# Keys and first centring by token in 64x64 quarters of the array, in two rounds with the banks exchanged between them

## The chip, the core and the metric

The kernel runs on one core of one Trainium2 chip. The metric is the device time of one execution, in microseconds (us). Before the change three executions took 1174.82, 1178.27 and 1172.48 us, so the median is 1174.82 us. Lower is better.

## What is computed

The reference takes 32 images of 64 channels and 32 x 32 pixels, and applies three blocks one after the other. The parts that matter here are the layer norm that stands ahead of attention, and the keys:

```
x = x + conv_block(group_norm(x))            # gated 1x1 convolutions
t = tokens(x)                                # 1024 tokens of 64 features per image
u = (t - mean(t)) / sqrt(var(t) + 1e-5)      # per token, over its 64 features
q, k, v = u @ Wq, u @ Wk, u @ Wv             # 64 x 64 weights
Q, K = elu(q) + 1, elu(k) + 1
KV = sum over tokens of K (x) v, per head    # linear attention, 8 heads
t = t + (u + layernorm(relu([u, msg] @ W1) @ W2))       # msg = layernorm(attended @ Wm)
t = t + mixture_of_8_experts(layernorm(t))   # top 2 of 8, each 64 -> 128 -> 64, GELU
```

All of it is in 32-bit floats but for a few constants.

## The kernel before, in words

Two images lie on the 128 partitions together: image 0 of a pair on partitions 0 to 63, image 1 on 64 to 127, a feature per partition and 1024 tokens in the free dimension. Such a pair is a slot, two slots make a group, and there are 8 groups. A slot's matrix results go to one tensor R0 or R1, two PSUM banks of 512 columns each; the experts use two tensors of their own, HP0 and HP1.

The work is software-pipelined over groups. The steady list SCHEDULE names the dense stages of group a (convolution, attention, hidden layers, router), and between them it sets units of the experts of group a-1. For each unit TensorE runs a first layer (L847), ScalarE the GELU (L992), TensorE a second layer (L861), VectorE the weighting (L1355) and GpSimd the addition to the sum (L1044). Each engine walks the same list in order, so the list fixes the order on every engine, and semaphores fix the times. Group 0 and the convolution of group 1 (called EARLY in the code) have another list, OPENING, in which no expert unit stands. Groups 2 to 7 go through the steady list from their convolution on, groups 1 to 7 from the keys on.

Two stages make a result that is laid out by token, with 128 tokens on the partitions and 2 x 64 features in the columns. They do so by holding 128 x 128 of the data as weights and moving a 128 x 128 matrix past it, which has the 64 x 64 weights of both images on its diagonal and zeros elsewhere:

- `centre_1` (L699 by the helper `by_token`) subtracts each token's mean. It waits for VectorE's sum x1 (L1163), half a slot at a time. ScalarE squares the result (L945), VectorE adds the squares up (L1184), takes the reciprocal root in some ten short steps (L1190 on), and scales (L1210). The result is turned back to features by TensorE (L641).
- `key` makes the keys. It first fills half a slot with ones (L681, from bf16 constants, so that the result is k + 1), then adds the keys (L708), and waits half by half for VectorE's finished queries (L1243), because both lie in R. ScalarE takes the exponential (L958), VectorE the minimum and maximum (again L1243), and `key_value` (L717) starts when both halves of the slot's keys are done.

A 32-bit matmul of the program is two pairs of a weight load and a matmul record in the trace, each pair for half of its passes. Where a matmul uses 64 rows or 64 columns of the array, others can run in the rest of it. The query stage (L692) does this already with four quarters.

Of the kernel before, what the change touches and what calls it, by code (L numbers as in the profile page):

```python
# [10 lines left out]
BF16 = mybir.dt.bfloat16  # L11
ALU = mybir.AluOpType
ACT = mybir.ActivationFunctionType
AX_X = mybir.AxisListType.X

P = 128
C = 64
# [5 lines left out]
CH = 512  # L23
NCH = T // CH
# [32 lines left out]
NQ = CH // P  # L57
# [73 lines left out]
def build(nc, x, wpack, w1e, reps, out):  # L131
    xd = x.rearrange("(n two) c t -> n (two c) t", two=2)
    od = out.rearrange("(n two) c t -> n (two c) t", two=2)
    with ExitStack() as ctx:
        def sb(name, shape, dt=F32):
            return ctx.enter_context(nc.sbuf_tensor(name, shape, dt))
# [4 lines left out]
        def sems(name):  # L141
            return [sem(f"{name}{g}") for g in range(G)]
# [5 lines left out]
        XN = sb("XN", [P, G, T])  # L148
# [22 lines left out]
        SPAN = sb("SPAN", [P, NQ, P])  # L171
        BH = sb("BH", [P, 1])
        BT = sb("BT", [P, 1])
        ONE = sb("ONE", [P, 2], BF16)
        MINUS = sb("MINUS", [P, 1])
        BI = sb("BI", [P, 2, 2])
        W1E = sb("W1E", [P, E, HID])
# [7 lines left out]
        R = [psum(f"R{s}", T) for s in range(G)]  # L185
# [5 lines left out]
        def w(name, rows=slice(0, P)):  # L191
            a, n = COLS[name]
            return W[rows, a:a + n]
# [10 lines left out]
        def half(c):  # L204
            return slice(c * CH, (c + 1) * CH)
# [16 lines left out]
        def img(k):  # L222
            return slice(k * C, (k + 1) * C)
# [42 lines left out]
        x1_done = sems("x1_done")  # L266
        ln_ps = sems("ln_ps")
# [4 lines left out]
        xn_back = sems("xn_back")  # L272
        xs_done = sems("xs_done")
        msg_norm = sems("msg_norm")
        qk_ps = sems("qk_ps")
        qk_exp = sems("qk_exp")
        one_set = sem("one_set")
        qk_done = sems("qk_done")
# [28 lines left out]
        xf_done = sems("xf_done")  # L307
# [25 lines left out]
        def pieces(slots):  # L333
            return [(s, c) for s in slots for c in range(NCH)]
# [11 lines left out]
        def at(n, c):  # L346

            return (n - 1) * NCH + c + 1

        LAST = NCH - 1  # L350
# [209 lines left out]
        def _(pe):  # L560
            mm = nc.tensor.matmul
# [10 lines left out]
            def parts(a, b, par):  # L572
# [52 lines left out]
                def blocks(c):  # L625

                    return range(c * TB // NCH, (c + 1) * TB // NCH)

                def centre_1(slots):
                    for s, c in pieces(slots):  # L630
                        pe.wait_ge(x1_done[s], at(a + 1, c))
                        if a == EARLY:
                            pe.wait_ge(xf_done[s], at(a, c))
                        by_token(s, c, Xa, w("center")).then_inc(ln_ps[s], 1)

                def features_1(slots):

# [41 lines left out]
                def one_everywhere(s, c):  # L679

                    mm(R[s][:, half(c)], ONE[:, 1:2].broadcast_to([P, P]), ONE[:, 0:1].broadcast_to([P, CH]), start=True, stop=False)  # L681

# [10 lines left out]
                                          start=False, stop=True)  # L693
                            last.then_inc(qk_ps[s], 1)

                def by_token(s, c, src, weights):

                    for j in blocks(c):
                        last = mm(R[s][:, P * j:P * j + P], src[:, s, P * j:P * j + P], weights,  # L699
                                  start=True, stop=True)  # L700
                    return last

                def key(slots):
                    for s, c in pieces(slots):
                        pe.wait_ge(qk_done[s], at(a * 2 + 1, c))
                        one_everywhere(s, c)
                        for j in blocks(c):
                            last = mm(R[s][:, P * j:P * j + P], XN[:, s, P * j:P * j + P], w("wk"),  # L708
                                      start=False, stop=(j == blocks(c)[-1]))
                        last.then_inc(qk_ps[s], 1)  # L710

                def key_value(slots):
                    for s in slots:
# [180 lines left out]
        def _(act):  # L894
# [5 lines left out]
            f(BT[:, :], BI[:, 1, 0:1], ACT.Copy, scale=0.5).then_inc(act_prep, 1)  # L900
            act.wait_ge(act_prep, 2)
            f(ONE[:, 0:1], BI[:, 0, 0:1], ACT.Copy, bias=1.0, scale=0.0)
            f(ONE[:, 1:2], BI[:, 0, 0:1], ACT.Copy, bias=1.0 / P, scale=0.0).then_inc(one_set, 1)

            def parts(a, b, par):
# [558 lines left out]
```

## Time and profile before

| | |
|---|---|
| median of the runs, us | 1174.82 |
| span of the profiled execution, us | 1171.7 |
| TensorE busy | 1058.5 us, 90% |
| VectorE, ScalarE, GpSimd busy | 63%, 55%, 31% |
| mean granted TensorE clock | 0.985 |
| centring records L699 | 256, in 8 stretches |
| key records L708, fill records L681 (queries' fill too) | 256, 64 |

Of the profiled execution the trace gives the span, from the first instruction to the last; the runs' times are taken around the whole execution, and their median is 3.1 us longer. The span, and each stage in it, is what the rows speak of. The stages of groups 2 to 7 repeat every 138.2 us to within 0.02 us, so one group stands for six.

### The profile page before, as it was taken

What the parts mean: (1) busy time and instruction counts of PE and PEld (TensorE: products, weight loads), DVE (VectorE), ACT (ScalarE), POOL (GpSimd) and SP (SyncE); (2) the same over time, 40 slices, a digit from 0 to 9 for tenths busy, and PEclk for the clock granted to TensorE, in tenths of its full rate; (3) what the DMA queues carried; (4) which work ended last, traced back from release to release, by engine and by line L of the source; (5) the groups of instructions that cost most, each with busy time, mean ns of one, the idle gap of its engine ahead of it and who ended that gap; (6) DMA issues with size and microseconds to landing.
All of it is one profiled execution on the core that took longest, in us unless ns stands there. A gap on an engine that the chain in (4) does not pass through costs nothing.

```text
span 1171.7 us, 16823 instructions
## 1 busy us (share of the span) xinstructions
PE 1058.5 (90%) x6646; PEld 442.3 (38%) x6646; DVE 740.2 (63%) x1529; ACT 641.8 (55%) x866; POOL 361.7 (31%) x280
## 2 busy tenths in 40 slices
PE   4798589979999899988999899998999989998898
PEld 1453244323533245332453235432453324532232
DVE  5744745686647875587664966468764886556344
ACT  3345355654566556664556546556556555665454
POOL 0000031333323333333232333133332342324465
PEclk9989889999999999999999999999999999999999
DMA  5000086007700284005810068000850039200760
GB/s 157 6 1 1 1 179 149 3 22 173 169 1 19 54 189 104 1 19 112 185 50 1 19 149 198 1 19 19 194 134 1 18 69 201 42 1 19 179 145 23
DMA packets 15597, 88.62 MB, mean 76 GB/s; under 512 B 3488, under 2 KB 6816, under 8 KB 11424
## 3 DMA queue, kind: packets, MB, share of 16 engines
q1 hardware_dynamic: 15520, 87.57, 32.3%
q8 instruction: 52, 0.85, 0.3%
q14 instruction: 25, 0.20, 0.1%
HBM read 78.12 MB, written 9.44 MB: 75 GB/s over the span
## 4 chain that ended last, share of the span: by engine, by line
PE 74%; DVE 12%; ACT 9%; issue 3%; DMA 1%; DVEq 0%; POOL 0%; POOLq 0%; SPq 0%
PE HP L847 15%; PE HP L861 14%; ACT H L992 5%; PE R L646 5%; PE R L621 4%; PE R L610 4%; PE R L699 3%; PE R L717 2%; PE R L708 2%; PE R L786 2%; PE R L795 2%; PE R L788 2%; PE R L861 2%; PE R L675 2%; DVE TM L1355 2%
## 5 line engine op out<-in xcount | busy, mean ns | idle before, releaser
L1044 POOL TENSOR_TENSOR XB<-TM,XB 128x512 f32<-128x512 f32 x254 | 323.0, 1286 | 658.5 <-DVE TM L1355 658.5
L992 ACT ACTIVATE H<-HP,W 128x1024 f32<-128x1024 f32 x224 | 243.0, 1116 | 205.7 <-PE HP L847 205.1
L1355 DVE SCALAR_TENSOR_TENSOR TM<-HP,B2S,CWB 128x512 f32<-128x512 f32 x224 | 163.2, 742 | 207.1 <-PE HP L861 196.3
L847 PE MATMUL HP<-XF,W1E 64*128 64x512 f32 x1024 | 269.9, 630 | 19.3 <-DVE TM L1355 18.5
L861 PE MATMUL HP<-H,W 128*64 128x512 f32 x896 | 233.1, 616 | 18.0 <-ACT H L992 18.0
L847 PEld LDWEIGHTS HP<-XF,W1E 64*128 64x128 f32 x1024 | 84.1, 187 | 143.9 <-DVE TM L1355 71.0
L861 PEld LDWEIGHTS HP<-H,W 128*64 128x64 f32 x896 | 48.5, 135 | 171.2 <-ACT H L992 116.3
L1156 DVE SCALAR_TENSOR_TENSOR BIG<-R,T 128x512 f32<-128x512 f32 x112 | 69.5, 681 | 20.9 <-PE R L610 20.8
L930 ACT ACTIVATE T<-R 128x512 f32<-128x512 f32 x96 | 57.4, 598 | 39.8 <-PE R L646 31.4
L958 ACT ACTIVATE T<-R,MINUS 128x512 f32<-128x512 f32 x64 | 41.4, 688 | 27.3 <-PE R L708 24.4
L1243 DVE SCALAR_TENSOR_TENSOR BIG<-T,R 128x512 f32<-128x512 f32 x64 | 41.8, 684 | 21.6 <-ACT T L958 21.6
L610 PE MATMUL R<-IM,REP 32*128 32x512 f32 x336 | 50.2, 482 | 5.1 <-ACT T L918 2.3
L621 PE MATMUL R<-BIG,W 128*64 128x512 f32 x224 | 53.0, 617 | 1.9 <-DVE BIG L1156 1.9
L975 ACT ACTIVATE BIG<-R,BH 128x512 f32<-128x512 f32 x64 | 40.5, 683 | 21.7 <-PE R L788 21.7
L1035 POOL TENSOR_TENSOR XB<-XN,X 128x1024 f32<-128x1024 f32 x14 | 33.2, 2396 | 54.9 <-ACT XN L953 54.9
L992 ACT ACTIVATE BIG<-HP,W 128x1024 f32<-128x1024 f32 x32 | 33.9, 1110 | 26.0 <-PE HP L847 26.0
L1355 DVE SCALAR_TENSOR_TENSOR TM<-R,B2S,CWB 128x512 f32<-128x512 f32 x32 | 24.0, 751 | 37.8 <-PE R L861 35.1
L924 ACT ACTIVATE T<-R,W 128x512 f32<-128x512 f32 x28 | 19.2, 687 | 45.5 <-PE R L621 45.5
L1163 DVE TENSOR_TENSOR X<-X,T 128x512 f32<-128x512 f32 x28 | 21.6, 773 | 32.4 <-ACT T L924 32.4
L1218 DVE SCALAR_TENSOR_TENSOR T<-R,T 128x512 f32<-128x512 f32 x64 | 40.4, 682 | 1.9 <-PE R L675 1.7
L918 ACT ACTIVATE T<-R 128x512 f32<-128x512 f32 x56 | 29.1, 602 | 21.4 <-PE R L610 21.3
L610 PEld LDWEIGHTS R<-IM,REP 32*128 32x128 f32 x336 | 21.7, 202 | 48.1 <-issue 19.6
(179 smaller groups left out, 1411.3 us busy)
## 6 DMA issues: line engine op xcount, KB each, us to landing
CWB<-gates_hbm SPq DMA_DIRECT2D x32, 1536.0 KB, 20.4
CWB<-gates_hbm SPq DMA_DIRECT2D x32, 512.0 KB, 6.6
out<-XB SPq DMA_DIRECT2D x15, 512.0 KB, 3.0
X<-x SPq DMA_DIRECT2D x14, 512.0 KB, 3.8
XF<-x SPq DMA_DIRECT2D x2, 512.0 KB, 6.1
gates_hbm<-RT SPq DMA_DIRECT2D x16, 64.0 KB, 1.6
W<-wpack SPq DMA_DIRECT2D x1, 968.0 KB, 4.9
W1E<-w1e SPq DMA_DIRECT2D x1, 512.0 KB, 7.4
```

The costliest lines, as they stand in the source:

```text
L610: last = mm(Ra[s][:, half(c)], REP[rows, n, :], IM[rows, s, part, :], start=(part == 0), stop=(part == 1))
L621: last = mm(Ra[s][img(k), half(c)], w("ow")[:, C * h:C * h + C], BIGa[:, s, 2 * k + h, half(c)], start=(h == 0), stop=(h == 1))
L646: return mm(R[s][:, half(c)], weights, src[:, s, half(c)], start=True, stop=True)
L847: last = mm(HP[u % BATCH][:, half(k)], W1E[img(k), e, :], XF[img(k), 1 - par, s, half(c)], start=True, stop=True)
L861: last = mm(sums_of(b, u)[img(k), :], w("w2e")[:, C * e:C * e + C], activated(b, u)[:, k, :], start=True, stop=True)
L930: f(T2[:, s, half(c)], R[s][:, half(c)], ACT.Square).then_inc(ln_sq[s], 1)
L958: f(T1[:, s, half(c)], R[s][:, half(c)], ACT.Exp, bias=MINUS[:, :]).then_inc(qk_exp[s], 1)
L992: f(activated(b, u).rearrange("p k t -> p (k t)"), HP[u % BATCH][:, :], ACT.Gelu, bias=col(B1E + e))\
L1044: nc.gpsimd.tensor_tensor(acc, TM[:, u % BATCH, :], acc, ALU.add).then_inc(acc_done, 1)
L1156: v.scalar_tensor_tensor(out=BIGa[:, s, 2 * k + h, half(c)], in0=Ra[s][:, half(c)], scalar=1.0, in1=T2a[:, s, half(c)], op0=ALU.add, op1=A ...
L1243: v.scalar_tensor_tensor(out=dst[s][:, half(c)], in0=T1[:, s, half(c)], scalar=1.0, in1=R[s][:, half(c)], op0=ALU.min, op1=ALU.max).then_i ...
L1355: v.scalar_tensor_tensor(out=TM[:, u % BATCH, :], in0=sums_of(b, u), scalar=B2S[:, e % 2, e // 2:e // 2 + 1], in1=CWB[:, s, e, half(c)], o ...
```

## The change

`by_token` now works on a whole slot, in quarters of the array. A matmul holds 64 tokens of one image (64 x 64) and moves that image's own 64 x 64 weights. Eight blocks of 128 tokens, two images and two halves of a block make 32 matmuls per slot instead of 8 of 128 x 128. In the first of two rounds image 0 (array rows 0 to 63) writes the first bank of R and image 1 (rows 64 to 127) the second; in the second round the banks are exchanged. Between the rounds TensorE waits for its own last matmul of the first round, by a new semaphore. Both callers now wait for both halves of a slot before they begin, and both halves of the result are announced together at the end. The fill of the keys is done in quarters as well, with a new constant 1/64.

```
                 def centre_1(slots):
-                    for s, c in pieces(slots):
-                        pe.wait_ge(x1_done[s], at(a + 1, c))
+                    for s in slots:
+                        pe.wait_ge(x1_done[s], at(a + 1, LAST))
                         if a == EARLY:
-                            pe.wait_ge(xf_done[s], at(a, c))
-                        by_token(s, c, Xa, w("center")).then_inc(ln_ps[s], 1)
+                            pe.wait_ge(xf_done[s], at(a, LAST))
+                        by_token(s, Xa, w("center"), c1_first[s], True).then_inc(ln_ps[s], NCH)
...
-                def by_token(s, c, src, weights):
-                    for j in blocks(c):
-                        last = mm(R[s][:, P * j:P * j + P], src[:, s, P * j:P * j + P], weights,
-                                  start=True, stop=True)
+                def by_token(s, src, weights, first_round, alone):
+                    for turned in range(2):
+                        if turned:
+                            pe.wait_ge(first_round, a + 1)
+                        for q in range(NQ):
+                            for k in range(2):
+                                at_block = P * (NQ * (k ^ turned) + q)
+                                for n in range(2):
+                                    last = mm(R[s][img(n), at_block + C * k:at_block + C * k + C],
+                                              src[img(k), s, at_block + C * n:at_block + C * n + C], weights[img(k), img(k)],
+                                              start=alone, stop=alone or (turned == 1 and q == NQ - 1))
+                        if not turned:
+                            last.then_inc(first_round, 1)
                     return last
                 def key(slots):
-                    for s, c in pieces(slots):
-                        pe.wait_ge(qk_done[s], at(a * 2 + 1, c))
-                        one_everywhere(s, c)
-                        for j in blocks(c):
-                            last = mm(R[s][:, P * j:P * j + P], XN[:, s, P * j:P * j + P], w("wk"),
-                                      start=False, stop=(j == blocks(c)[-1]))
-                        last.then_inc(qk_ps[s], 1)
+                    for s in slots:
+                        pe.wait_ge(qk_done[s], at(a * 2 + 1, LAST))
+                        for c in range(NCH):
+                            for n in range(2):
+                                mm(R[s][img(n), half(c)], ONE[img(c), 2:3].broadcast_to([C, C]), ONE[img(c), 0:1].broadcast_to([C, CH]),
+                                   start=True, stop=False)
+                        by_token(s, XN, w("wk"), key_first[s], False).then_inc(qk_ps[s], NCH)
...
+            f(ONE[:, 2:3], BI[:, 0, 0:1], ACT.Copy, bias=1.0 / C, scale=0.0)
```

On TensorE, in the steady list, the keys stood like this before, from the first wait for the queries of slot 1 to the sum of keys times values (L681 fill, L708 keys, L717 keys times values; a semaphore's name ends in its slot):

```order
L681 MATMUL R<-ONE 128x512 [waits qk_done1]
L708 MATMUL R<-W,XN 128x128 x4
L681 MATMUL R<-ONE 128x512 [waits qk_done1]
L708 MATMUL R<-W,XN 128x128 x4
L681 MATMUL R<-ONE 128x512 [waits qk_done0]
L708 MATMUL R<-W,XN 128x128 x4
L681 MATMUL R<-ONE 128x512 [waits qk_done0]
L708 MATMUL R<-W,XN 128x128 x4
L717 MATMUL R<-BIG 128x130 [waits ones_set1,qk_done1]
```

The same place on TensorE in the changed kernel (L720 fill, L708 again the keys, L729 keys times values):

```order
L720 MATMUL R<-ONE 64x512 [waits qk_done1]
L720 MATMUL R<-ONE 64x512 x3
L708 MATMUL R<-W,XN 64x64 x16
L708 MATMUL R<-W,XN 64x64 [waits key_first1]
L708 MATMUL R<-W,XN 64x64 x15
L720 MATMUL R<-ONE 64x512 [waits qk_done0]
L720 MATMUL R<-ONE 64x512 x3
L708 MATMUL R<-W,XN 64x64 x16
L708 MATMUL R<-W,XN 64x64 [waits key_first0]
L708 MATMUL R<-W,XN 64x64 x15
L729 MATMUL R<-BIG 128x130 [waits ones_set1,qk_done1]
```

Per slot there are 32 small matmuls for 8, 4 fills for 2, one wait for the queries for two, and a wait on the engine itself in the middle. The first centring in the steady list, on TensorE, before (L699 the centring, L847 the next expert layer):

```order
L699 MATMUL R<-W,X 128x128 [waits x1_done1]
L699 MATMUL R<-W,X 128x128 x3
L699 MATMUL R<-W,X 128x128 [waits x1_done1]
L699 MATMUL R<-W,X 128x128 x3
L699 MATMUL R<-W,X 128x128 [waits x1_done0]
L699 MATMUL R<-W,X 128x128 x3
L699 MATMUL R<-W,X 128x128 [waits x1_done0]
```

And after, up to the expert layer that follows (L859):

```order
L708 MATMUL R<-W,X 64x64 [waits x1_done1]
L708 MATMUL R<-W,X 64x64 x15
L708 MATMUL R<-W,X 64x64 [waits c1_first1]
L708 MATMUL R<-W,X 64x64 x15
L708 MATMUL R<-W,X 64x64 [waits x1_done0]
L708 MATMUL R<-W,X 64x64 x15
L708 MATMUL R<-W,X 64x64 [waits c1_first0]
L708 MATMUL R<-W,X 64x64 x15
L859 MATMUL HP<-XF,W1E 128x512 [waits comb_done,xf_done0]
```

No stage changes its place among the others, on any engine. ScalarE has one more instruction, for the constant, at the start.

## Rows read from the trace of the kernel before

**Rows 1.** The page: span, busy time, and the chain that ended last.

```profile
span 1171.7 us, 16823 instructions
...
PE 1058.5 (90%) x6646; PEld 442.3 (38%) x6646; DVE 740.2 (63%) x1529; ACT 641.8 (55%) x866; POOL 361.7 (31%) x280
...
PE 74%; DVE 12%; ACT 9%; issue 3%; DMA 1%; DVEq 0%; POOL 0%; POOLq 0%; SPq 0%
```

**Rows 2.** Timeline, TensorE, first centring: start us, length us, instruction, count, idle before.

```profile
289.95 3.84 PE L699 MATMUL R<-W,X 128*128 128x128 f32 x32
293.72 1.99 PE L847 MATMUL HP<-XF,W1E 64*128 64x512 f32 x8
296.06 2.08 PE L861 MATMUL HP<-H,W 128*64 128x512 f32 x8 [0.36 <-ACT H L992]
298.14 1.25 PE L641 MATMUL R<-W,BIG 128*128 128x128 f32 x8
```

**Rows 3.** The same stretch on VectorE and ScalarE.

```profile
290.79 0.69 DVE L1163 TENSOR_TENSOR X<-X,T 128x512 f32<-128x512 f32 x1 [0.65 <-ACT T L924]
...
293.83 0.60 ACT L945 ACTIVATE T<-R 128x512 f32<-128x512 f32 x1 [0.30 <-PE R L699]
...
294.46 0.69 DVE L1184 TENSOR_REDUCE SM<-T 128x8 f32<-128x512 f32 x1 [0.21 <-ACT T L945]
...
297.39 1.29 DVE L1210 TENSOR_TENSOR BIG<-R,SM 128x512 f32<-128x512 f32 x2
```

**Rows 4.** Timeline, TensorE, from the keys to the keys times values.

```profile
308.72 0.39 PE L681 MATMUL R<-ONE 128*128 128x512 bf16 x1
308.94 1.05 PE L708 MATMUL R<-W,XN 128*128 128x128 f32 x8
...
313.15 3.75 PE L717 MATMUL R<-BIG 128*128 128x130 f32 x32
```

**Rows 5.** The same stretch on ScalarE and VectorE, queries first.

```profile
305.55 2.42 ACT L958 ACTIVATE T<-R,MINUS 128x512 f32<-128x512 f32 x4
...
310.04 0.69 ACT L958 ACTIVATE T<-R,MINUS 128x512 f32<-128x512 f32 x1 [2.06 <-PE R L708]
...
307.52 2.47 DVE L1243 SCALAR_TENSOR_TENSOR BIG<-T,R 128x512 f32<-128x512 f32 x4
310.76 0.69 DVE L1243 SCALAR_TENSOR_TENSOR BIG<-T,R 128x512 f32<-128x512 f32 x1 [0.77 <-ACT T L958]
...
314.08 0.69 DVE L1243 SCALAR_TENSOR_TENSOR BIG<-T,R 128x512 f32<-128x512 f32 x1 [0.42 <-ACT T L958]
```

**Rows 6.** One line each: durations in ns (min/median/max), first and last start.

```profile
L708 PE MATMUL R<-W,XN x256: 272/275/275, 63.3 to 1004.1; 128*128 128x128 f32 x128
...
L675 PE MATMUL R<-BIG,SPAN x32: 270/270/372, 336.0 to 336.9; 32*128 32x128 f32 x32
...
L728 PE MATMUL R<-T,W x4: 169/210/250, 317.1 to 318.5; 128*128 128x1 f32 x4
...
L692 PEld LDWEIGHTS R<-XN,W x16: 129/131/133, 303.1 to 304.7; 64*64 64x64 f32 x16
L692 PE MATMUL R<-XN,W x16: 589/614/641, 303.1 to 305.1; 64*64 64x512 f32 x16
```

**Rows 7.** Timeline, TensorE, cut off at 336.05 us: L675's records begun by then.

```profile
336.03 0.39 PE L675 MATMUL R<-BIG,SPAN 32*128 32x128 f32 x4 [0.15 <-DVE BIG L1206]
```

**Rows 8.** Timeline of the queries on TensorE, in quarters.

```profile
303.08 1.09 PE L692 MATMUL R<-XN,W 64*64 64x512 f32 x8
304.10 0.61 PE L681 MATMUL R<-ONE 128*128 128x512 bf16 x2
```

**Rows 9.** Timeline of group 0, centring: TensorE, VectorE's x1, and its last sum.

```profile
45.10 3.84 PE L699 MATMUL R<-W,X 128*128 128x128 f32 x32
...
45.82 1.29 DVE L1163 TENSOR_TENSOR X<-X,T 128x512 f32<-128x512 f32 x2
...
49.61 0.69 DVE L1184 TENSOR_REDUCE SM<-T 128x8 f32<-128x512 f32 x1 [0.21 <-ACT T L945]
```

**Rows 10.** Timeline of group 0, keys times values, on TensorE.

```profile
68.31 3.75 PE L717 MATMUL R<-BIG 128*128 128x130 f32 x32
```

More of the change, by code:

```diff
@@ L173, in build @@
         BT = sb("BT", [P, 1])
-        ONE = sb("ONE", [P, 2], BF16)
+        ONE = sb("ONE", [P, 3], BF16)
         MINUS = sb("MINUS", [P, 1])
@@ L274, in build @@
         msg_norm = sems("msg_norm")
+        c1_first = sems("c1_first")
+        key_first = sems("key_first")
         qk_ps = sems("qk_ps")
```

## The prediction, made before the changed kernel ran

> **What bounds the kernel now.** I read the page's busy shares and chain first, then the timeline of the two stages on three engines, then single lines for what a small matmul costs. TensorE is busy 1058.5 of 1171.7 us, and the chain that ended last is 74% TensorE, 12% VectorE and 9% ScalarE [rows 1]. So most of what TensorE saves should count, but not all: near both changed stages the chain leaves TensorE. The first centring of a steady group runs 32 records in a row, from 289.95 until L847 follows at 293.72 [rows 2]. Behind it VectorE works without a pause from the last sum of squares (294.46) through the root steps to L1210 at 297.39, whose first half releases L641 at 298.14 [rows 2, 3]. TensorE has then just ended L861, so at L641 the two paths are about even. The keys take TensorE from 308.72 to 313.15, again without a gap [rows 4]; exponential and minimum/maximum follow each half, and the last half's VectorE step starts at 314.08 [rows 5], hidden today behind L717 of the other slot.
>
> **TensorE's own time.** In today's keys a half slot is 1.11 us (308.72 to 313.15 is four of them): a fill of 0.22 (308.72 to 308.94) and 8 records in 0.89, so 111 ns per record of 128 moved columns [rows 4]; centring is 32 such records, 3.57 us and the change to the next tiling. After the change a slot has 64 records of 64 columns, four at a time. If the quarters really run together, four records take what one record of 64 columns takes, half of 111: 56 ns. That they can is seen in the queries: 8 records of 512 columns in four quarters need 1.02 us (303.08 to 304.10), where one after the other each would be 4 x 111 ns, 3.6 us in all [rows 4, 8]. A weight load of 64 x 64 lasts 131 ns as a record [rows 6], but overlaps in the same way. What no row shows is the rate at which the sequencer delivers: 56 ns for four pairs is 14 ns per pair. Bounds: four neighbours in different row strips start within 23 ns of each other (336.03, with the cut at 336.05), at most 8 ns apiece [rows 7], and over 32 records L675 ran at 28 ns each (0.9 us from first to last start) [rows 6]. In the latter the array itself was the limit (111 ns for four), so 28 is a bound from above, no measured limit of delivery. I take 14, since neighbours at 8 ns show that pairs can come faster, and keep 28 for the range.
>
> The Trainium skill speaks against this value. Its page "TensorE: Matmul & The Clock Gate", section "Wait — 56ns, not 53.3ns?", says that starts never come closer than about 25 ns however small the matmul, and that with hardware decode off about 62 ns go to each. The trace has four starts within 23 ns, so as a distance between neighbours the 25 does not hold here; as a mean rate over many records no row refutes it. By 62, L675 could hardly have kept 28. By 25 the round would take 0.80 us instead of 0.45; what that does to the time is the second rival.
>
> The wait between the rounds: the last record of round 1 must finish. A record of 128 columns lasts 275 ns and one of a single column 169, so one of 64 some 222 [rows 6]. Release takes 0.03 to 0.04 us (ScalarE ends at 310.73, VectorE starts at 310.76 [rows 5]). Then the first load isn't hidden: L692's first records are 52 ns longer than its others (641 to 589) [rows 6]. From the last start of round 1 to the first of round 2: 0.31 us. Nothing else is in flight; L847 and all stages behind it wait with it. Below, the cost can hardly be under 0.22 (the record itself); above I allow 0.6. A round is 7 x 56 + 20 = 0.41 us from first to last start, so from a slot's first record to its last 1.13, its result is there at 1.35, and the next slot can start at 1.18. Fill for a slot: four bf16 matmuls in four quarters, 0.22 for 0.44. Per group TensorE then needs 2.36 for 3.57 (centring) and 2.80 for 4.43 (keys), 2.8 us less, 23 us over 8 groups. That is not what arrives.
>
> **Keys, steady group.** The queries' four VectorE steps start at 307.52 and are 0.60 apart, so slot 1's second half ends at 308.80 [rows 5]. Today TensorE starts at 308.72 on the first half; now at 308.84. Fill to 309.06, last record starts at 310.20, result at 310.42. ScalarE 310.46, its second half 0.58 later (four in 2.42 [rows 5]); VectorE 311.18 and 311.78, end 312.47. L717 is released at 312.51 with an unhidden load of 0.10 (first L675 records 372 for 270 ns [rows 6]), so effectively 312.61. TensorE has the second slot's keys done by about 311.65 (its queries ended at 309.99, in time) and waits 0.8 us: the wait that replaces the work. Today L717 is at 313.15, so **0.54 us earlier**, not 1.6. Slot 0's keys end on VectorE at 313.9, before L717 of slot 1 ends at 314.4. The change of tiling ahead of L717 falls into that wait. Everything behind L717 follows in order, so I let the 0.54 pass on. Seven groups: 3.8 us.
>
> **First centring, steady group.** Slot 1 starts as today at 289.95, since both its halves were ready, and ends at 291.13. Slot 0 now waits for its second half: VectorE ends at 291.48 [rows 3], a new idle 0.4 us. First record effectively at 291.57, result at 292.92. ScalarE's second half then starts near 293.47 (0.51 behind the first, an estimate from 0.60 each with overlap), VectorE's second sum at 294.20 (two, 0.60 apart, from 293.59), against 294.46 [rows 3]: **0.26 us earlier**. TensorE's own L847 starts 0.9 us sooner but meets the GELU behind ScalarE's squares, and L641 needs L1210. Six groups: 1.5 us.
>
> **Opening.** Group 0's centring: slot 1's x1 is done at 45.82 + 1.29 = 47.11 [rows 9]; start 47.2, result 48.57, last sum from 49.84 instead of 49.61 [rows 9]: 0.2 us later. Its keys, by the steady working, free L717's second half 0.5 earlier than today (68.31 + 1.79 [rows 10]). Group 1's centring is paced by VectorE's x copies, 0.60 apart: nothing. Together 0.3 us gained.
>
> **Sum.** 3.8 + 1.5 + 0.3 = 5.6 us off the profiled execution: span 1171.7 to 1166.1. The runs' median is 3.1 above the span, so 1174.8 - 5.6 = **1169.2 us**. The added constant, and the 3,000 or so more TensorE records, I cost at nothing: the constant is ahead of any use, the records' code must be fetched in time behind long matmuls; if it is not, it belongs to the second rival.
>
> **The rivals.**
>
> First, the wait between rounds costs 0.6 instead of 0.31. One such wait stands on the path per changed stage (slot 0's in centring, slot 1's in keys): 0.3 x 15 = 4.4 us back, 1173.6. For it: no row has TensorE waiting for itself. Against: each part has its row.
>
> Second, slower than before: pairs come at 28 ns instead of 14. A round lasts 0.87 and the slot 2.05 to its last start. Centring: slot 1 holds TensorE to 292.04, slot 0 ends near 294.1 with its result at 294.3; last sum at 295.6, 1.1 late. Keys: both slots take TensorE to 313.5, and slot 0's keys end on VectorE at 315.7, so its L717 starts at 315.8 for 314.94, 0.9 late. 6 x 1.1 + 7 x 0.9 + 2 (opening) = 15: 1190 us. At 25 ns, by proportion, 1185 or so; I give that end a third of this rival's chance. Between the two values centring breaks even near 17 ns per pair and the keys near 19; from 18 on the change loses. For it: nothing in the trace ever sustained under 28. Against: the neighbours' starts.
>
> Third, the path moves as TensorE moves, and the 23 us all arrive: 1152. Against: VectorE's step starts 0.03 behind ScalarE's end in both stages.
>
> Fourth, nothing arrives: the earlier L717 and L641 are eaten by another wait in the same 138 us, 1174.8. Against: the order is fixed and TensorE idles little.
>
> **How the numbers follow.** Chances: forecast 0.60, long wait 0.09, slow pairs 0.17, all arrives 0.06, nothing arrives 0.08. About 0.5% (5.9 us) is what a measurement tells from no change; my forecast lies almost on that edge, so its 0.60 goes 0.32 to faster and 0.28 to same. Faster 0.32 + 0.06 = 0.38; same 0.28 + 0.09 + 0.08 = 0.45; slower 0.17. The forecast's own range is 1165 to 1173 (0.1 us of error in a slot's path is 1.5 us). For 8 in 10 I go down to 1163 and up to 1181, which takes in the waits and part of the slow pairs.
>
> **What would show it.** In the profile after: 32 centring records of a slot within 0.45 us per round, a gap of 0.31 between rounds; TensorE idle 0.8 us ahead of keys times values with VectorE as releaser, and 0.4 us ahead of slot 0's centring; keys times values released 5.0 us behind the first VectorE step of the queries (307.52 to 313.15 is 5.6 today). TensorE busy down by about 20 us against a span down by 6. I am wrong if a round takes over 0.57 us (18 ns per pair), or if the gap is over 0.6, or if the stages shift and the 138.2 us period does not.

## The result, and the profile after

The changed kernel is slower: 1178.71 us median (1176.77 to 1184.53, 20 runs) against 1174.70 for the kernel before (1170.93 to 1178.83, 20 runs), a ratio of 1.0041 with a 95% interval of 1.0029 to 1.0053 (the ratio weighs all runs; the two medians alone give 1.0034). The forecast was 1169.2. By the bound of 0.5% this is still "no change", but the sign is wrong and the size is off by 9.5 us, so the interest lies in where the forecast 5.6 us went.

The page of the changed kernel, beside [rows 1] (PE is TensorE, PEld its weight loads, DVE VectorE, ACT ScalarE, POOL GpSimd; PEclk is the granted TensorE clock in tenths of full speed; "issue" is time in which an engine waits for nothing that the profile shows; q8 is the DMA queue that carries instructions):

```profile
span 1175.4 us, 19958 instructions
...
PE 1043.3 (89%) x8214; PEld 421.7 (36%) x8214; DVE 736.2 (63%) x1529; ACT 638.7 (54%) x867; POOL 361.2 (31%) x280
...
PEclk8798889999999999999999999999999999999999
...
q8 instruction: 65, 1.06, 0.4%
...
PE 67%; DVE 17%; ACT 10%; issue 4%; DMA 1%; DVEq 0%; POOL 0%; POOLq 0%; SPq 0%
```

TensorE is busy 15.2 us less than the 1058.5 of before, and yet the span is 3.7 us longer. VectorE and ScalarE did the same work, but for the one instruction more on ScalarE. The chain gave seven points of TensorE to VectorE (12 to 17%), ScalarE and "issue" (3 to 4%). The queue that carries instructions brought 65 packets of 16 KB (1.06 MB by 65) where the kernel before needed 52:

```profile
q8 instruction: 52, 0.85, 0.3%
```

First a group in which the change works. The last group's keys in the changed kernel, timeline of TensorE, its weight loads (PEld) and VectorE, beside [rows 4, 5]:

```profile
1002.73 2.47 DVE L1256 SCALAR_TENSOR_TENSOR BIG<-T,R 128x512 f32<-128x512 f32 x4
...
1004.06 0.41 PE L720 MATMUL R<-ONE 64*64 64x512 bf16 x4
1004.09 0.71 PEld L708 LDWEIGHTS R<-W,XN 64*64 64x64 f32 x32
1004.30 1.43 PE L708 MATMUL R<-W,XN 64*64 64x64 f32 x64
1005.03 0.56 PEld L708 LDWEIGHTS R<-W,XN 64*64 64x64 f32 x32 [0.23 <-PE R L708]
...
1005.55 0.40 PE L720 MATMUL R<-ONE 64*64 64x512 bf16 x4
...
1007.85 2.39 PE L729 MATMUL R<-BIG 128*128 128x130 f32 x19 [0.66 <-DVE BIG L1256]
```

A slot's 64 records start within 1.21 us, and the loads of the second round stretch over 0.56 us. With 0.13 for the last load, 0.43 is left for 32 starts: waves of four 58 ns apart (7 x 58 plus some 20 ns inside the last). The matmul records of a round start within 0.42 to 0.48 us: waves are 57 to 58 ns apart, but in two of the four rounds the second follows the first by 106. The records themselves put 0.32 us between the last start of round 1 and the first of round 2, of which the row's [0.23] is what the loader shows as idle. The next slot begins 1.49 us behind (1004.06 to 1005.55). The keys times values (L729) are released 5.12 us behind the first query step of VectorE, for 5.63 before (307.52 to 313.15 in [rows 4, 5]). TensorE waits 0.66 us there, for VectorE. All this is as the forecast had it.

Now the same place one group later than the rows shown of before, in group 3. Timeline of TensorE in the changed kernel:

```profile
447.68 0.41 PE L720 MATMUL R<-ONE 64*64 64x512 bf16 x4
447.92 1.43 PE L708 MATMUL R<-W,XN 64*64 64x64 f32 x64
449.16 0.40 PE L720 MATMUL R<-ONE 64*64 64x512 bf16 x4
449.38 1.41 PE L708 MATMUL R<-W,XN 64*64 64x64 f32 x60
453.37 0.33 PE L708 MATMUL R<-W,XN 64*64 64x64 f32 x4 [2.58 <-issue]
```

Four records before the end of the keys, TensorE stands still for 2.58 us in the middle of a round, with its operands present, on "issue": it waits for nothing that the profile shows. Four others stand in the same trace, in the keys or the keys times values of groups 1, 2, 4 and 5:

```profile
175.43 2.98 PE L729 MATMUL R<-BIG 128*128 128x130 f32 x13 [2.54 <-issue]
...
313.86 2.39 PE L729 MATMUL R<-BIG 128*128 128x130 f32 x19 [0.65 <-issue]
...
592.54 0.46 PE L708 MATMUL R<-W,XN 64*64 64x64 f32 x16 [0.74 <-issue]
...
730.87 0.68 PE L708 MATMUL R<-W,XN 64*64 64x64 f32 x28 [0.89 <-issue]
```

Together 7.40 us. The kernel before has no such wait of over 0.4 us behind 130 us. The two long ones cost more than their length, as busy time by stretch shows (columns: stretch and its length, busy us and records of five engines, granted clock, DMA share, GB/s):

```profile
447.00:449.20 2.20, 2.04 (x76) 1.22 (x76) 1.82 (x4) 0.00 (x0) 2.20 (x2) 1.00 0.88 179
...
453.30:454.80 1.50, 1.43 (x14) 1.36 (x14) 0.34 (x1) 1.06 (x2) 0.00 (x0) 1.00 0.92 289
454.80:458.20 3.40, 3.40 (x18) 3.40 (x18) 2.99 (x5) 2.60 (x3) 1.27 (x1) 0.51 0.09 34
458.30:461.00 2.70, 2.70 (x20) 1.87 (x20) 0.81 (x4) 0.72 (x2) 0.00 (x0) 1.00 0.00 0
```

1.5 us behind the end of the wait the granted clock falls from 2.4 to 1.2 GHz (0.51 in the row) for 3.4 us, at full TensorE load, and 18 matmuls run there where 20 run in the next 2.7 us. The same comes with the wait of 2.54 that ends at 175.43: there the clock falls at 174.99, 0.4 us before the wait is over and 2.1 behind its beginning, and single L729 records lengthen from 272 to 423 ns. With the three waits of under 0.9 us it does not happen. At half the clock at most half of a stretch is lost, 1.7 us of 3.4, so the two cost up to 3.4 us.

**What the five waits share.** I counted what the trace holds of TensorE (loads, matmuls and its semaphore instructions) from the start to the first one behind each wait: 2497, 4545, 6593, 8641, 10689. They lie exactly 2048 apart, which is 8 x 256, while a steady group has 2072: the waits do not stand at a fixed place of the stage but 24 records (some 12 matmuls) earlier in each group. A packet of the instruction queue is 16 KB, 256 instructions if one has 64 bytes, and the counts fit TensorE's alone. Each count is 193 above a multiple of 256; behind record 193 the changed kernel has 16,439 records left, which fill 65 pieces of 256, and the kernel before 13,305, which fill 52. Those are the numbers of packets, and it comes out so in all thirteen traces of this case (a matmul whose record is missing counted by its load). The Trainium skill, page "Advanced Engine Details and Errata", section "ISA Cache", says that an engine's code comes in lines of 16 KB, 256 instructions, and that there are only two (beside which it gives 128 KB for TensorE). The trace agrees with the first; how many lines TensorE holds, no run here shows.

So I cut TensorE's records into pieces of 256 that end at these counts, and looked for the packet that starts while a piece runs. Here "used" is a piece's length without the wait at its end:

| wait at | its length | piece begun at | used in | packet starts, behind the piece's beginning |
|---|---|---|---|---|
| 175.43 | 2.54 us | 167.24 | 5.7 us | 5.59 us |
| 313.86 | 0.65 us | 308.62 | 4.6 us | 2.55 us |
| 453.37 | 2.58 us | 447.71 | 3.1 us | 2.87 us |
| 592.54 | 0.74 us | 586.20 | 5.6 us | 3.65 us |
| 730.87 | 0.89 us | 723.01 | 7.0 us | 5.12 us |

Each wait ends 2.6 to 2.8 us behind the start of its packet. TensorE ran out of code. The same count over all thirteen traces leaves no exception: behind 130 us they have 705 such boundaries between pieces. 17 show a wait on issue of over 0.4 us, each 193 records above a multiple of 256, and it ends 2.5 to 2.9 us behind the start of the packet; at each of the other 688 the packet had started at least 2.6 us before. The keys of a group are 272 of its records (136 matmuls and as many loads) in 3.1 us; before, they were 72 in 4.4 us. A piece that begins at or shortly before this stretch can be used up before the next is there. In the kernel before, packets start as late (3.6 us behind the piece begun at 306.14, 9.5 behind that of 175.44), but there no piece behind 130 us is used in less than 14.5 us.

### The profile page after: what moved, and what is told of

It reads as the page before. It is cut to its first block, busy times and chain, and to the rows that moved or that the text cites. A ratio compares the mean times of both kernels' runs of the same rounds, so it can differ in the third digit from the quotient of the medians.

```text
span 1175.4 us, 19958 instructions
## 1 busy us (share of the span) xinstructions
PE 1043.3 (89%) x8214; PEld 421.7 (36%) x8214; DVE 736.2 (63%) x1529; ACT 638.7 (54%) x867; POOL 361.2 (31%) x280
## 3 DMA queue, kind: packets, MB, share of 16 engines
q8 instruction: 65, 1.06, 0.4%
## 4 chain that ended last, share of the span: by engine, by line
PE 67%; DVE 17%; ACT 10%; issue 4%; DMA 1%; DVEq 0%; POOL 0%; POOLq 0%; SPq 0%
PE HP L859 13%; PE HP L873 13%; PE R L649 5%; ACT H L1005 5%; PE R L623 4%; PE R L612 4%; PE R L798 2%; PE R L729 2%; PE R L800 2%; PE R L807 2%; PE R L678 2%; PE R L873 2%; DVE TM L1368 2%; PE R L708 2%; PE R L665 2%
## 5 line engine op out<-in xcount | busy, mean ns | idle before, releaser
L859 PE MATMUL HP<-XF,W1E 64*128 64x512 f32 x1024 | 271.5, 634 | 19.4 <-DVE TM L1368 18.5
L859 PEld LDWEIGHTS HP<-XF,W1E 64*128 64x128 f32 x1024 | 84.5, 187 | 144.1 <-DVE TM L1368 71.0
L729 PE MATMUL R<-BIG 128*128 128x130 f32 x256 | 35.0, 296 | 6.2 <-issue 3.2
```

Source lines behind the costliest of these rows:

```text
L729: last = mm(R[s][:, 0:VW], K[s][:, P * j:P * j + P], V[s][:, j, :], start=(j == 0), stop=(j == TB - 1))
L859: last = mm(HP[u % BATCH][:, half(k)], W1E[img(k), e, :], XF[img(k), 1 - par, s, half(c)], start=True, stop=True)
```

## The experiments

Theory A: code delivery. The stage is as fast as forecast, and the loss is the waits on the next piece of code, with the clock that the long ones take along. It needs both a dense piece of code and a delivery made late by other transfers. Rivals: the tiling itself (the 64 x 64 quarters, or the two rounds) costs more than it brings; the half clock comes first; chance.

A ratio compares the runs with those of the kernel before on the same chip. It weighs all of them, with a 95% interval in brackets, and is not the quotient of the two medians. "Period" is the distance between a steady group's first record with the weights W1X (the hidden layers' first matmul) and the next group's, in a group with neither a wait on issue nor a half-clock stretch. Before it is 138.2 us. In the changed kernel the last one (896.1 to 1033.5) is of that kind, and it is 137.4.

**The changed kernel again.** No edit.

> The changed kernel once more, as the yardstick of this series. Code theory (TensorE's instructions come in pieces of 256, 16 KB each, by DMA queue 8; between the two quarter-tiled key slots one piece is used up faster than the next can come while the gate weights' transfer fills the DMA engines): ratio to before 1.002 to 1.006, and in the profile TensorE idle ended by issue in the keys or at the start of keys times values in 4 to 6 of the 7 steady groups, each time 2.6 to 2.8 us after a queue-8 packet starts, at record 193 of a piece. Clock theory (the quarter-tiled records let the granted clock fall): the low-clock stretches would stand in the keys themselves before any idle time.

Measured: 1181.37 us (6 runs) against 1173.39 (29), ratio 1.0059 (1.0038 to 1.0081). The waits stand at the same records: 176.25 (2.51 us), 314.84 (0.64), 453.01 (2.34), 593.50 (0.99), 732.83 (0.88). Chance does not do that. This and the next three ran together.

**Keys by token only.** The centring is put back to whole blocks.

```diff
-                    for s in slots:
...
+                    for s, c in pieces(slots):
...
-                        by_token(s, Xa, w("center"), c1_first[s], True).then_inc(ln_ps[s], NCH)
+                        whole_blocks(s, c, Xa, w("center")).then_inc(ln_ps[s], 1)
```

> Keys in quarters and two rounds as in the changed kernel, first centring as before. Code theory: per steady group some 96 x 2 TensorE instructions fewer than the changed kernel, so the boundaries of the pieces wander by about 200 of 256 per group instead of standing still at the end of the keys; one to three of the seven groups stall, not five, and without stalls each keys stage gives 0.4 to 0.5 us: ratio 0.996 to 1.001. Rival (the quarter-tiled keys are slow by themselves, or the clock falls with them): as slow as the changed kernel, ratio about 1.004.

Measured: 1174.66 us (12 runs), ratio 1.0039 (1.0009 to 1.0070), period 137.6. Two waits, both in the keys: 451.47 (2.30 us) and 867.01 (0.82). The period and the waits fit theory A. The ratio is higher than it allowed, though the two medians differ by only 0.11%: five of the 12 runs took 1178 to 1186 us, the other seven 1170.7 to 1174.9, and the profiled run is one of the short ones. The long ones had a lower mean granted clock, 0.959 to 0.968 for 0.971 to 0.982, so they hold more half-clock time; what set it off, and whether more waits stand in them, was not seen.

**Centring by token only.** The keys are put back.

```diff
...
-                        by_token(s, XN, w("wk"), key_first[s], False).then_inc(qk_ps[s], NCH)
...
+                        one_everywhere(s, c)
+                        for j in blocks(c):
+                            last = mm(R[s][:, P * j:P * j + P], XN[:, s, P * j:P * j + P], w("wk"),
+                                      start=False, stop=(j == blocks(c)[-1]))
+                        last.then_inc(qk_ps[s], 1)
```

> First centring in quarters and two rounds, keys as before. Code theory: no stall, since long matmuls stand on both sides of the centring; by the profile of the changed kernel a steady group gains 0.15 us, six groups 0.9 us, group 0 loses 0.3: ratio 0.998 to 1.001. Rival (late release of slot 0's centring costs more than it saves): 1.001 to 1.003.

Measured: 1173.85 us (12 runs), ratio 0.9996 (0.9981 to 1.0010), period 138.04, no wait on issue. The centring stage is dense too (128 records of each kind in 3 us), but no piece ran out there. One piece of 3.0 us lies wholly in a centring (begun at 843.04), and the packet of the next had started 2.0 us before it, at 841.04. Its own gain, 0.16 us a group, is too small for the ratio to show.

**Code moved by 128 instructions, at the start.** 32 matmuls of one column, each of four instructions, ahead of everything. They are no part of the result.

```diff
+            for _ in range(32):
+                mm(HP[1][0:32, 0:1], w("wim")[:, 0:32], w("wim")[:, 0:1], start=True, stop=True)
```

> The changed kernel with 128 TensorE instructions more ahead of everything (32 tiny matmuls while the inputs are on their way), which moves every later boundary between pieces of code by half a piece. Code theory: the boundary stands between the two key slots instead of at both ends, half a piece is already there, and the stalls of 0.6 to 2.6 us in groups 1 to 5 shrink to under 0.5 each: 5 to 7 us faster than the changed kernel, ratio to before 0.996 to 1.000. Rivals (work, waits between rounds, DMA load or clock by themselves): no change, ratio 1.004, since the work is the same.

Measured: 1172.20 us (12 runs), ratio 0.9980 (0.9961 to 0.9999), period 137.4. The five waits are gone; one of 0.49 us stands at 1004.53. TensorE has more work, the stages have the same tiling, and the kernel is some 9 us faster than the changed kernel beside it. The opening is put back: group 0's queries begin at 62.3 us, for 58.4 in the kernel before and 56.7 in the changed one. The added matmuls wait for the first weights, but the half-clock stretches of the opening differ too, so how much is theirs is not shown.

**Narrow gate transfers in the changed kernel.** The other half of the theory: what makes the delivery late. During the keys the DMA engines bring the gate weights for the combine. From group 1 on only 64 of their 1024 columns are brought; the rest of the combine then uses old values, which leaves that part of the computation out.

```diff
-                            rows = gates_hbm[s, E * k:E * k + E, :][experts]
-                            sp.dma_start(CWB[img(k), s, experts, :],
...
+                            t = T if a == 0 else C
+                            rows = gates_hbm[s, E * k:E * k + E, 0:t][experts]
+                            sp.dma_start(CWB[img(k), s, experts, 0:t],
...
```

> The changed kernel, in which from the second group on only 64 of 1024 columns of the gate weights are brought (the result uses old weights there), so that the DMA engines are nearly free while the keys run. Code theory in its sharper form (the next piece of code is late because its packets wait among the gate weights' packets): stalls in groups 2 to 5 gone or under 0.3 us, that in group 1, whose loads are whole, stays near 2.5; 3 to 5 us faster than the changed kernel, ratio to before 0.998 to 1.002. If a piece is late by the mere rate of use, the DMA load being beside the point: stalls as in the changed kernel, ratio 1.004 to 1.006.

Measured: 1171.61 us (10 runs) against 1174.88 (35), ratio 0.9978 (0.9957 to 1.0000), period 137.4. Timeline of TensorE in this kernel, first its one wait, under the transfer that was left whole, then group 3:

```profile
170.21 2.39 PE L730 MATMUL R<-BIG 128*128 128x130 f32 x19 [0.66 <-DVE BIG L1257]
175.04 2.48 PE L730 MATMUL R<-BIG 128*128 128x130 f32 x13 [2.44 <-issue]
...
445.49 0.41 PE L721 MATMUL R<-ONE 64*64 64x512 bf16 x4
445.73 1.43 PE L709 MATMUL R<-W,XN 64*64 64x64 f32 x64
446.97 0.40 PE L721 MATMUL R<-ONE 64*64 64x512 bf16 x4
447.19 1.43 PE L709 MATMUL R<-W,XN 64*64 64x64 f32 x64
```

And its busy time by stretch (columns as above), over both places:

```profile
168.00:175.00 7.00, 3.85 (x95) 3.43 (x84) 4.58 (x7) 4.93 (x6) 1.26 (x1) 1.00 0.89 217
443.00:448.00 5.00, 4.68 (x118) 2.37 (x118) 3.20 (x6) 2.39 (x5) 3.68 (x3) 1.00 0.01 3
```

This run is the clearest. The code is the same and its pieces begin at the same records. With the DMA share at 0.01, the wait of 2.58 us in group 3 is gone, though that piece is again used in under 3 us; its packet starts 0.1 us ahead of the piece, not 2.9 behind it. In group 2 it starts 0.8 us behind the piece for 2.6, and in groups 4 and 5 it starts 2.5 and 1.2 us ahead for 3.7 and 5.1 behind. With 0.89, in group 1, packet and wait stand as before (5.55 us behind, 2.44 us). Groups 2, 4 and 5 lost their waits.

**Narrow gate transfers in the kernel before.** The same edit, as the control.

> The kernel before with the same reduced gate weights' load, the yardstick for the last one. No stall either way; if the load doesn't slow anything else, ratio 0.998 to 1.001. Then the quarter-tiled version with reduced load would, by the code theory, lie at or below it apart from group 1's stall.

Measured: 1175.93 us (10 runs), ratio 1.0004 (0.9980 to 1.0028). The lighter transfers alone bring nothing that these runs can tell. This and the next two ran with the narrow gates.

**Code moved by 128, in idle time.** The 32 small matmuls now stand behind the first group's routing, where TensorE has no hurry.

```diff
+                    if a == 0:
+                        for _ in range(32):
+                            mm(HP[1][0:32, 0:1], w("wim")[:, 0:32], w("wim")[:, 0:1], start=True, stop=True)
```

> As the shifted kernel, but the 128 instructions stand in TensorE's idle stretch of 9 us in the opening (behind the turning of the gates' logits), so that they can't delay the start. Code theory: stalls as in the shifted kernel (none over 0.5 us), and the start as in the changed kernel: 1 to 4 us faster than the shifted one, ratio to before 0.994 to 0.998. Rival (the shifted kernel gained by a later or denser start): back at 1.003 or above.

Measured: 1168.09 us (12 runs), ratio 0.9944 (0.9925 to 0.9964): faster than both kernels. Group 3's keys in its timeline, and its line of the keys among the groups by line:

```profile
441.65 1.43 PE L708 MATMUL R<-W,XN 64*64 64x64 f32 x64
442.89 0.40 PE L720 MATMUL R<-ONE 64*64 64x512 bf16 x4
443.11 1.43 PE L708 MATMUL R<-W,XN 64*64 64x64 f32 x64
445.20 3.85 PE L729 MATMUL R<-BIG 128*128 128x130 f32 x32 [0.67 <-DVE BIG L1259]
```

```profile
L708 PE MATMUL R<-W,XN 64*64 64x64 f32 x1024 | 21.3, 221 | 1.5
```

The changed kernel's own group reads

```profile
L708 PE MATMUL R<-W,XN 64*64 64x64 f32 x1024 | 22.2, 221 | 5.7 <-issue 4.2
```

Here the transfers are whole: a stretch over these keys (441 to 447 us) has a DMA share of 0.60. No wait on issue of over 0.4 us is left behind 130 us, the period is 137.4, and TensorE is busy 1039.1 us in a span of 1165.1. (A wait of 0.2 us is left at 998.71, in group 7.) Against the changed kernel's profiled execution that is 10.3 us, and 7.40 of waits plus up to 3.4 of half clock behind the two long ones is up to 10.8. In group 1 the parts can be seen one by one: its W1X stage starts 4.2 us earlier than in the changed kernel (196.0 for 200.3), which is the wait of 2.54 and 1.7 of half clock.

**The keys in one round.** On top of the last kernel, the keys go in one round without the change of banks, and VectorE writes them out in the other order instead.

```diff
-                        by_token(s, XN, w("wk"), key_first[s], False).then_inc(qk_ps[s], NCH)
+                        for j in range(TB):
+                            for k in range(2):
+                                for n in range(2):
+                                    last = mm(R[s][img(n), CH * k + C * j:CH * k + C * j + C],
+                                              XN[img(k), s, P * j + C * n:P * j + C * n + C], w("wk")[img(k), img(k)],
+                                              start=False, stop=(j == TB - 1))
+                        last.then_inc(qk_ps[s], NCH)
```

> As the last one, but the keys go in one round: image 0 always to the first bank, image 1 to the second, no wait in the middle; VectorE puts the halves back into the old order as it writes K. By the profile of the changed kernel the gap between rounds is 0.32 us, of which one per group is on the path: 0.25 to 0.3 us per group, 2 us in all, ratio about 0.002 under that of the shift in the idle stretch. Rival: denser use of code brings stalls back, or VectorE's write in pieces of 64 costs more than it saves (over 0.1 us a piece): same or slower than the shift in the idle stretch.

Measured: 1172.15 us (1163.48 to 1173.68, 12 runs), ratio 0.9963 (0.9939 to 0.9988), higher than expected. Locally it does what it should, in the timeline of TensorE:

```profile
450.73 0.41 PE L719 MATMUL R<-ONE 64*64 64x512 bf16 x4
450.97 1.10 PE L724 MATMUL R<-W,XN 64*64 64x64 f32 x64
451.93 0.41 PE L719 MATMUL R<-ONE 64*64 64x512 bf16 x4
452.16 1.10 PE L724 MATMUL R<-W,XN 64*64 64x64 f32 x64
454.21 1.05 PE L734 MATMUL R<-BIG 128*128 128x130 f32 x7 [0.94 <-DVE BIG L1268]
...
1005.81 2.50 PE L734 MATMUL R<-BIG 128*128 128x130 f32 x20 [0.66 <-issue]
```

From the first fill to L734 are 3.48 us, for 3.79 in the kernel with two rounds (441.41 to 445.20): the 0.31 of the change of banks. The period falls to 137.1. But one wait on issue has come back (0.66), and the profiled run, among the longer ones, has half-clock stretches at 263 (6.8 us), 403 and 816 (3.4 each), where the kernel with two rounds had two of 3.4, at 670 and 946. Three of the 12 runs stand at 1163.5 to 1166.1, below all but two of the 12 runs of the two-round kernel. Whether the clock falls there by chance or by the new timing was not settled.

**Code moved by 64.** The same edit with range(16). This and the last two ran together.

> The changed kernel with 16 tiny matmuls (64 TensorE instructions, no part of the result) put behind the first group's routing; the run before had 32 (128 instructions). Theory of code delivery: a boundary between two 256-instruction pieces no longer falls 193 records into a group's keys but 64 records earlier, so the dense stretch is shared by two pieces; counted on the trace with narrow gates, the densest pieces that begin so in the key stages of groups 1 and 2 last 6.3 and 7.8 us where the stalled ones lasted 4.4 and 2.7. At most two waits on issue of over 0.4 us behind 130 us, none of over 1 us, steady period 137.4 us, ratio 0.993 to 0.997, profiled span under 1171. Rival (the 128-instruction shift helped by something else, such as the extra TensorE work at that place, with no role for where the pieces end): half the added work gives half the gain, ratio about 0.999, with waits left in groups 1 and 3.

Measured: 1169.17 us (12 runs) against 1175.08 (23), ratio 0.9965 (0.9941 to 0.9988), period 137.4. Two waits, in groups 1 and 2, in the timeline of TensorE the second:

```profile
312.31 1.08 PE L708 MATMUL R<-W,XN 64*64 64x64 f32 x40
314.58 0.58 PE L708 MATMUL R<-W,XN 64*64 64x64 f32 x24 [1.20 <-issue]
```

Half the added work brought more than half of the gain, and the waits moved: in group 2 from L729's ninth record back to L708, in group 3 there is none. The ratio and the number of waits came as theory A had them. That none would be over 1 us did not hold (0.89 and 1.20), nor did a profiled span under 1171: it was 1176.8. That execution is one of three of the 12 at 1178.6; the other nine took 1166.6 to 1173.4. Its opening has a half-clock stretch of 13.7 us at 92, and two of 6.8 us stand at 402 and 542 and two of 3.4 at 683 and 959. So density alone does not give the length of a wait: one needs the start of the packet too (2.2 and 5.2 us behind pieces used in 4.2 and 6.9).

**The kernel before, code moved by 128.** The control for the last three.

> The kernel before with the same 32 tiny matmuls behind the first group's routing. Theory of code delivery: the kernel before has no wait on issue of over 0.4 us behind 130 us, so moving the piece boundaries has nothing to remove: ratio 0.999 to 1.001, steady period 138.2 us, no such wait. Rival (the added matmuls help by themselves, by keeping TensorE busy or its clock up): ratio about 0.995, as far below 1 as in the changed kernel with them.

Measured: 1173.71 us (12 runs), ratio 0.9994 (0.9980 to 1.0009), no wait on issue of over 0.4 us behind 130 us, period 138.2. The small matmuls help only where there is a wait to remove.

**Code moved by 128, a second time.**

> The changed kernel with 32 tiny matmuls behind the first group's routing, a second time, beside the two above on one chip. Theory of code delivery: no wait on issue of over 0.4 us behind 130 us, steady period 137.4 us (0.8 below the kernel before), ratio 0.993 to 0.996 as the first time. Rival (the first result was a lucky draw of half-clock stretches): ratio 0.998 or more.

Measured: 1169.78 us (6 runs), ratio 0.9950 (0.9930 to 0.9969), no such wait, period 137.4. The gain repeats.

**Verdict.** Theory A stands on three legs: waits at a fixed record count, gone when the pieces begin elsewhere, and gone with the same code when the DMA engines are free. The tiling rival falls by the period (137.4 for 138.2) and by the run that moves the code and keeps the tiling. The clock rival falls as the cause: where the clock drops at a long wait, it drops after the wait has begun, never ahead of it, and it goes with the wait. Not shown is why a packet starts when it does, other than that a free DMA path makes it start earlier. The starts of the W1X stage, from the traces, show the account:

| kernel | group 1 | group 7 | six periods | waits on issue in them |
|---|---|---|---|---|
| before | 198.3 | 1030.0 | 831.6 | none |
| changed | 200.3 | 1033.5 | 833.2 | four, 4.9 us |
| changed, code moved by 128 | 196.0 | 1023.0 | 827.0 | none |

Without the waits six groups gain 4.6 us, 0.77 each; the forecast was 0.80. (Each of the two has 6.8 us at half clock in these six periods.)

## Why the prediction was wrong

**The step that failed** is the last sentence of the sum: the added TensorE records "I cost at nothing: [...] the records' code must be fetched in time behind long matmuls". It is not fetched in time. The long matmuls do stand ahead of the stage, but a piece of 256 instructions that covers it is used in 3.1 to 7.0 us, and its successor's packet starts 2.6 to 5.6 us behind the piece's beginning. The profile before had what was needed to doubt it: 52 packets of code, a gate transfer over the same stage, and an edit that puts 272 records into 3.1 us. I knew the number of added records and never asked how fast one piece would be used. The term was 0 and measured 7.4 us of waits, plus up to 3.4 of half clock. I also gave a failure here to the second rival, a steady rate of 28 ns a pair. That is another mechanism: the pairs come at 14.5 ns and then stop.

**The other steps,** each by the runs:

| step | forecast | measured |
|---|---|---|
| four records in quarters | 56 ns | 58 ns |
| last start of round 1 to first of round 2 | 0.31 us | 0.32 us |
| slot to slot, keys, with fill | 1.40 us | 1.48 to 1.49 us |
| keys times values behind the first query step | 5.0 us | 5.12 us |
| TensorE's new wait for VectorE there | 0.8 us | 0.66 us |
| keys, gain a group | 0.54 us | 0.51 at L729, 0.64 by the keys-only period |
| centring, gain a group | 0.26 us | 0.15 to 0.16 |
| TensorE busy | 20 us less | 15.2 less; 19.4 with the code moved |
| whole, without waits on issue | 5.6 us off | 6.8 and 5.3 off (medians with the code moved) |

The rates rested on [rows 6 to 8], and they held. The Trainium skill's rule that starts never come closer than about 25 ns (page "TensorE: Matmul & The Clock Gate", section "Wait — 56ns, not 53.3ns?") does not hold here as a mean rate either: 32 matmul records, in four quarters of the array, start in 0.42 to 0.48 us. The rival of slow pairs falls with it, and so does the long wait between rounds.

**Centring** was the term that I sized too high; the keys brought a little more than forecast (0.64 for 0.54), which nearly makes up for it. In the last group of the changed kernel:

```profile
985.31 3.06 PE L708 MATMUL R<-W,X 64*64 64x64 f32 x128
...
988.44 1.08 ACT L958 ACTIVATE T<-R 128x512 f32<-128x512 f32 x2 [0.50 <-PE R L708]
989.07 1.28 DVE L1197 TENSOR_REDUCE SM<-T 128x8 f32<-128x512 f32 x2 [0.31 <-ACT T L958]
...
993.35 1.26 PE L644 MATMUL R<-W,BIG 128*128 128x128 f32 x8 [0.62 <-DVE BIG L1223]
```

From the first centring record to the back-turn (L644) are 8.04 us, for 8.19 before ([rows 2], 289.95 to 298.14). ScalarE gets slot 0 at 3.13 us behind the first record, where I had 2.97 and the release: some 0.1 late, and half of the small gain is gone. TensorE's wait for VectorE at the back-turn went up in turn, from 6.1 us over the execution to 10.0. The opening's 0.3 us can't be told: the half-clock stretches of the first 150 us differ from run to run.

**The chances.** "Nothing arrives" (1174.8) and "slow pairs" (1190) were the rivals nearest to the result, one by its time, the other by its sign, and neither by its mechanism. The range (1163 to 1181) held the time because it reached for slow pairs. That is luck, not insight.

## What to carry to other kernels

Splitting matmuls into small quarters buys array time with instructions, and those have a delivery of their own. Before such a change, count the loads and matmuls of the densest stage against its length and ask what the DMA engines do in it: here 256 of them used in 3 to 7 us beside a transfer could cost 0.5 to 2.6 us, and used in over 7 us they never did. Waits on "issue" in the middle of a row of equal matmuls, at record counts that differ by multiples of 256, are its mark. A few small matmuls in idle time that move the boundaries are a cheap remedy (ratios of 0.995 and 0.994 here, for 1.004 and 1.006), but a brittle one, since every edit ahead of the stage moves them again.

## What the runs showed of the hardware that I had not expected

- TensorE's code arrives by a DMA queue in packets of 16 KB. Beside transfers it is the start of the packet that is late, by several us, more than its length: the packets ahead of the waits took 1.1 to 1.4 us each; the queue's share over 20 us around the keys of group 3 is 0.8% of 16 engines for two packets (1.3 us each) in the changed kernel, 0.6% (1.0 us) with narrow gates.
- Each of the six waits on code of 2.3 to 2.6 us in these traces came with 3.4 us at 1.2 GHz, which began between 0.4 us before the end of the wait and 1.5 behind it; the eleven of 0.5 to 1.2 us came with none.
- fp32 matmuls of 64 x 64 with 64 columns in four quarters start 58 ns apart by fours (the second four of a round often 106 behind the first), and four neighbours 3 to 8 ns apart.
- Half-clock stretches of 3.4 or 6.8 us come and go between executions of one kernel at about 400, 540, 675 and 820 us. They lengthen a period by 0.9 to 1.4 us (3.4 us long) or about 2.3 (6.8 us long) and blur any ratio by more than the centring's gain. What sets them off was not tried.
